# Adjacency product with residual and layer norm: groups of 4 rows in two ring slots instead of groups of 5 in three

## What is computed

```python
keep = (u >= 0.1).astype(x.dtype)
x_drop = x * keep / (1.0 - 0.1)
x = _layernorm(x + jnp.matmul(adj, x_drop), axis=-1)     # over 64 columns, eps 1e-5
```

## Time and profile before

| | |
|---|---|
| median of 3 runs (lowest to highest) | 641.93 us (641.93 to 641.95) |
| profiled execution: its time, its span | 642.16 us, 640.2 us |
| TensorE matmul, weight load, VectorE, ScalarE busy | 80%, 41%, 9%, 3% |
| HBM read, written; mean rate over the span | 272.63 MB, 2.10 MB; 429 GB/s |
| mean granted TensorE clock | 0.906 of full speed |

### The profile page before, as it was taken

The page is one execution under the profiler, slowest core; times in us unless marked ns, Lnnn a source line. Parts: engine busy times, 40 slices in busy tenths (PEclk is TensorE's granted clock), DMA queues, the critical chain, the costliest instruction groups (busy, mean ns, idle before and its releaser), DMA issues.

```text
span 640.2 us, 7695 instructions
## 1 busy us (share of the span) xinstructions
PE 510.8 (80%) x3458; PEld 263.7 (41%) x3458; DVE 60.8 (9%) x268; ACT 17.0 (3%) x24; POOL 1.1 (0%) x8
## 2 busy tenths in 40 slices
PE   0088798798788787887788878878977977979997
PEld 0044444444443443443444434433433443445435
DVE  1200100100100100010100110010010020020202
ACT  0000000000000000000000000000000000000000
POOL 0000000000000000000000000000000000000000
PEclk9997988988988987989978978978977987979999
DMA  9999999999999999999999999999999999999998
GB/s 385 430 431 447 427 430 450 430 430 447 434 430 424 445 434 404 430 434 439 430 434 447 430 430 450 430 430 440 436 434 399 458 438 407 435 424 431 434 419 354
DMA packets 7348, 274.80 MB, mean 429 GB/s; under 512 B 944, under 2 KB 1072, under 8 KB 1456
## 3 DMA queue, kind: packets, MB, share of 16 engines
q1 hardware_dynamic: 7200, 274.70, 99.5%
q10 hardware_dynamic: 144, 0.03, 0.0%
HBM read 272.63 MB, written 2.10 MB: 429 GB/s over the span
## 4 chain that ended last, share of the span: by engine, by line
DMA 66%; PE 33%; issue 0%; SPq 0%; DVE 0%; ACT 0%; ACTq 0%; DVEq 0%
DMA adj_ring<-adj_blocks 66%; PE acc L234 31%; PE tail_acc L234 2%; PE back L241 0%; SPq L151 0%; PE final L273 0%; SPq L153 0%; DVE x_and_u L342 0%; SPq L172 0%; ACT std L224 0%; DVE acc_sb L280 0%; ACTq L202 0%; DVE stats L336 0%; DVE mean_var L338 0%; DVE rstd L340 0%
## 5 line engine op out<-in xcount | busy, mean ns | idle before, releaser
L234 PE MATMUL acc<-adj_ring,x_and_u 128*64 128x320 f32 x3072 | 463.9, 467 | 99.4 <-ACTq L202 99.4
L234 PEld LDWEIGHTS acc<-adj_ring,x_and_u 128*64 128x64 f32 x3072 | 232.1, 148 | 326.2 <-ACTq L202 107.3
L280 DVE COPY acc_sb<-acc 128x320 f32<-128x320 f32 x24 | 10.7, 486 | 477.0 <-PE acc L234 477.0
L234 PE MATMUL tail_acc<-adj_ring,x_and_u 128*64 128x384 f32 (+1 forms) x256 | 29.1, 382 | 0.9 <-DMA adj_ring<-adj_blocks 0.8
L241 PE MATMUL back<-twofold,acc_sb 128*128 128x64 f32 x126 | 16.8, 280 | 11.9 <-DVE acc_sb L280 11.9
L196 ACT ACT_TABLE_LOAD x10 | 12.8, 1283 | 502.5 <-DMA adj_ring<-adj_blocks 502.5
L241 PEld LDWEIGHTS back<-twofold,acc_sb 128*128 128x128 f32 x126 | 15.0, 191 | 18.8 <-DVE acc_sb L280 18.7
L234 PEld LDWEIGHTS tail_acc<-adj_ring,x_and_u 128*64 128x64 f32 x256 | 15.7, 137 | 13.9 <-issue 9.8
L311 DVE TENSOR_SCALAR x_and_u<-summed,mean,rstd 128x64 f32 (+1 forms) x63 | 15.2, 310 | 0.5
L248 PE MATMUL final<-x_and_u,identity 128*128 128x64 f32 x2 | 0.7, 434 | 13.2 <-DMA x_and_u<-xu 13.2
L289 DVE BATCH_NORM_STATS2 stats<-summed 128x6 f32<-128x64 f32 x63 | 9.3, 213 | 0.4
(11 more groups left out here) (17 smaller groups left out, 7.4 us busy)
## 6 DMA issues: line engine op xcount, KB each, us to landing
adj_ring<-adj_blocks SPq DMA_DIRECT2D x23, 7680.0 KB, 33.3
adj_ring<-adj_blocks SPq DMA_DIRECT2D x11, 5120.0 KB, 36.8
adj_ring<-adj_blocks SPq DMA_DIRECT2D x1, 5760.0 KB, 28.0
adj_ring<-adj_blocks SPq DMA_DIRECT2D x1, 4480.0 KB, 30.0
x_and_u<-xu SPq DMA_DIRECT2D x1, 4096.0 KB, 12.4
adj_ring<-adj_blocks SPq DMA_DIRECT2D x1, 3840.0 KB, 23.3
adj_ring<-adj_blocks SPq DMA_DIRECT2D x1, 3072.0 KB, 30.3
adj_ring<-adj_blocks SPq DMA_DIRECT2D x1, 2560.0 KB, 35.7
```

The source lines that it names most:

```text
L234: return nc.tensor.matmul(into[h * D:(h + 1) * D, 0:cols], x_drop[:, t * D:(t + 1) * D], adj_ring[:, at:at + cols], start=(t < 2), stop=(t ...
L280: last = nc.vector.tensor_copy(acc_sb[:, b * cols:(b + 1) * cols], part[:, 0:cols])
```

## The change

R goes from 5 to 4, and FULL from 12 to 15, so that the full groups are the same 60 rows. A k tile of a group then has 512 columns. The ring is 64 x 512 float32 = 128 KB per partition, in two slots of 32 k tiles (64 KB per partition each) instead of three of 24, 24 and 16. COLS is the whole TILE, so SPLIT is 1: one bank, and one matmul of 512 columns for each k tile. TAIL and LAST_TILES stay as they are.

```diff
-R = 5
-FULL = 12
+R = 4
+FULL = 15
 TILE = R * P
-SLOT_TILES = [24, 24, 16]
+SLOT_TILES = [32, 32]
...
-COLS = TILE // 2
+COLS = TILE
 SPLIT = TILE // COLS
```

## The result

The changed kernel takes **661.52 us** (median of 6 runs, 659.08 to 666.31), the kernel before 641.94 us in runs on the same chip (641.89 to 642.09). The ratio is 1.0307, with a 95% interval of 1.0284 to 1.0330. The forecast was 646.5 us, in a range of 643.9 to 649.0: the direction held, but the size was a quarter of what came, and the time lies outside the range. The scatter is new as well: 7 us between the runs of one kernel, where the kernel before has 0.2.

A forecast was written before the change was run, and what follows sets the result against it. Loads were taken to bound the kernel. To the profiled 642.16 us it added 3.9 (pause in the last full group) and 1.0 (late engine), less 0.3 (fewer transfers): 646.8, or 646.5 us against the median; range 643.9 to 649.0.

The forecast's parts named there:

- What bounds the kernel, and the race in each slot: Whole kernel: loads bound it; each slot races TensorE's time plus issue-to-data delay against the transfer still queued.
- TensorE's time for a slot: Each 32-tile slot: 13.65 us at full clock, 15.35 to 16.75 with half clock behind waits; 16.05 taken.
- The loop: no loss: Full groups' refills: first data at 16.6 to 18.0 us, before the 19.37 us transfer ends; 0 us lost.
- eats only its lead: Loop: engines finishing up to 2 us before the late one run dry in some slots, at no cost.
- The second rival: The loop stalls: up to 0.3 us on each of 28 refills, 8 us more, 655; chance 0.07.
- The last full group: Its second part waits for slot 2 with only 24 tiles queued: a pause of 3.9 us, 2.7 to 5.1.
- The late engine in the tail: Tail: an instruction fetch holds one engine, with no lead left after the pause; +1.0 us, 0 to 1.5.
- Fewer transfers: Main loads: 32 instead of 37 save their fixed part, 0.06 us each; -0.3 us.
- 64 KB steps: Rival, loop loads: partition runs 64 KB apart read slower, 420 instead of 433 GB/s; 17 us, 663; chance 0.05.

The follow-up runs named there:

- f4: The changed kernel with two more float32 matmuls of 512 columns in each slot, before its last pair; 676.44 us, ratio 1.0532.
- g1: The changed kernel with extra matmuls, 8 after slot 1 and 4 after turn_back, alternating between output-partition halves; 650.24 us, ratio 1.0108.
- h1: The changed kernel with 8 of the 32 k tiles of each slot left out of the products, all loads kept; 645.20 us, ratio 1.0043.
- g2: As g1, with the last full group in parts of 32, 16, 10 and 6 k tiles; 650.38 us, ratio 1.0144.
- e4: The changed kernel with three slots of 24, 24 and 16 k tiles instead of two of 32; 642.84 us, ratio 1.0012.
- e2: The changed kernel with four slots of 16 k tiles instead of two of 32; 643.96 us, ratio 1.0030.
- f2: The changed kernel with extra matmuls, 8 after slot 1 and 3 after turn_back, into one half of the output partitions; 655.20 us, ratio 1.0200.

## Why the prediction was wrong

**What bounds the kernel, and the race in each slot:** right. The loads bound it, and each slot is a race between TensorE's time plus a restart, and the transfer still queued.

**TensorE's time for a slot:** right, 13.95 to 16.84 us against 13.65 and 15.35 to 16.75. The half-clock phase behind the waits came as read from the earlier trace rows; at full clock 64 records take 13.98 us, 0.3 more than the 13.65 worked out.

**"The loop: no loss": this is the step that failed**, by 12 us. It has two faults. The first is the price of a restart. For the pause in the last group the working took 2.2 us from issue until the data flow; for the loop it took 1.0, the silence behind an issue. But silence is only the first piece of it: the first row of 32 KB on each engine is slow as well (1.4 to 2.2 us in the trace of before, where the later ones take 1.21), which is part of the 2.7 us that `xu` had over what its bytes take. In f4, where the queue runs quite dry, the first engine is back at its rate 1.4 to 1.5 us behind the issue and the last one 2.1 to 2.2, in most of its refills. The second fault is the sentence that an early engine which runs dry "eats only its lead". The lead of the first engine was put at 17.3 against 18.0 us, so the trace of before did say that it would run dry. What then happens is shown by the mean over the 16 engines: in the changed kernel they are all late by 13 us at the end of the loop, the first as much as the last, and the spread between them goes up and down between 0.5 and 2.9 us. Each short lead throws single engines back by up to 3 us, not always the ones in front; the slot is complete, and TensorE may start, only with the last; and as the engines drift apart, the first one has less lead at the next refill. This second fault is the one that costs: the last engine always had 2.2 us or more of lead, so a price of 2.2 us set against it would still have given no loss. The prediction named the sign of its own failure, slots landing over 19.5 us apart; they landed 19.8 us apart in the mean. The table above is the price that the working should have had: 15 of the 26 refills of the changed kernel had 2 us or less on the first engine, which costs 0.7 to 1.3 us each. Why single engines take up the new load so much later than the others, and why the packets behind a late issue are slow, no run here explains.

**The second rival** named the place and the mechanism ("each slot pays"), gave the point from which it decides as 2.4 us, and priced it at 8 us at most with a chance of 0.07. Its price came from the lead of the last engine alone.

**The last full group:** the pause came where it was forecast, and 3.8 us against 3.9 is partly luck, as two terms were off in opposite directions. The chain has TensorE's slot of 15.38 us, then SP's issue at 583.71 us; the second part took 13.7 us to land for 10.9 us of transfer, so 2.8 us for the restart, where 2.2 was taken and 2.7 was the upper end, while TensorE's slot was 0.7 us shorter than the 16.05 taken. With a shorter slot on TensorE the pause was 2.3 (g1) and 1.4 us (h1), with a first part as long as a slot 0.01 (g2).

**The late engine in the tail:** right in kind. The DMA view has a fetch at 635.3 us (packets, MB, share of 16 engines for 0.2 us; 1.1 us of one engine):

```profile
q8 instruction: 1, 0.02, 34.3%
```

and the tail piece then in flight lands 1.1 us late, against 1.0 forecast. A later small piece loses 0.8 more, with no fetch in sight; that is open.

**Fewer transfers:** fits, as the 0.4 us left over stand against 0.3; e4 and e2 give 0.09 and 0.07 us for each transfer more.

**64 KB steps:** no slowdown. The Trainium skill's rule on large steps between rows ("DMA: Bandwidth & Descriptors", section "Latency and other measured facts") was one of the rivals; h1's loads keep the steady 19.35 us at steps of 64 KB. The same section gives about 0.6 us to the first byte of a DMA of this kind. The trace agrees if it is counted from the end of the issuing instruction: at 466.32 us this took 0.33 us, and the first packet started at 467.28, 0.6 us behind its end and 1.0 us behind its start. But full flow took 1.5 to 2.2 us, and it is this figure that a queue about to run dry has to cover.

## What to carry to other kernels

A ring must be judged by the lead of its refills: what is queued behind the largest slot, less the compute engine's time for that slot, as the **first** of the 16 DMA engines sees it. Here 3.5 us of it cost next to nothing, 2 us 0.1 us a refill, and 1 to 2 us 0.7; three or four slots instead of two gave 8 to 21 us for 0.1 us a transfer. Where a working uses one restart price in one place and another elsewhere, it contradicts itself, and the dearer one should be tried everywhere before a "no loss" is written down.

No kernel here beats the kernel before, which keeps the queue full from its first load to its last.

## What the runs showed of the hardware

- A load queue that has run dry is back at its rate 1.4 to 1.5 us behind the issue on the first engine and 2.1 to 2.2 us on the last (f4). With 2 to 3 us of lead on the first engine single refills were still up to 0.6 us late.
- Behind a late issue packets of 64 KB took up to 4.2 us instead of 2.42 us (changed kernel); with the queue never dry none that started within 10 us behind an issue took over 2.5 us (h1).
- Rows of 64 KB go as one packet each, at the same 433 GB/s as rows of 60 and 40 KB.
- Extra matmuls into one half of the output partitions take twice as long as in alternating halves: 6.6 us and more for 16 records of 512 columns in f2, 3.4 in g1.
- In the changed kernel the granted clock fell to 0.50 (1.2 GHz) behind all of TensorE's waits of 3 us and more but one (of 3.63 us), and behind some of 2 to 3 us. With most waits cut to 1.6 to 2.0 us (g1) it fell in only six slots of the loop, behind waits of 1.96 to 3.5 us.
